# Attention stage of an audio tower: two batches of four product tiles a pair, head projections in another order

## The reference, cut to what matters

```
xn = LN(LN(h)) * ln_scale                       # h: [32, 250, 64]
Q, K, V = xn @ W_q[h], xn @ W_k[h], xn @ W_v[h] # 8 heads
q2, k2 = sum(Q*Q, -1), sum(K*K, -1)
sqdist = max(q2[..., :, None] + k2[..., None, :] - 2 Q K^T, 0)
out    = exp(-gamma * sqdist) @ V               # no normalisation by row
h      = h + concat_heads(out) @ W_o^T
```

## Time and profile before

| | us |
|---|---|
| median of 3 runs (lowest, highest) | 782.41 (780.72, 784.95) |
| the profiled execution | 780.68 |
| its span, first to last instruction | 778.5 |
| PE busy | 741.2 |
| DVE busy | 579.5 |
| ACT busy | 492.1 |
| POOL busy | 459.6 |

### The profile page before, as it was taken

The page is one execution under the profiler, slowest core; times in us unless marked ns, Lnnn a source line. Parts: engine busy times, 40 slices in busy tenths (PEclk is TensorE's granted clock), DMA queues, the critical chain, the costliest instruction groups (busy, mean ns, idle before and its releaser), DMA issues.

```text
span 778.5 us, 17037 instructions
## 1 busy us (share of the span) xinstructions
PE 741.2 (95%) x5712; PEld 435.2 (56%) x5712; DVE 579.5 (74%) x1474; ACT 492.1 (63%) x993; POOL 459.6 (59%) x620
## 2 busy tenths in 40 slices
PE   2999999999999999999999999999999999999994
PEld 1343356776667667676766666544555554454441
DVE  7676776677677676777767665788888888888864
ACT  1566777777767777777777777554554655545441
POOL 7645314654556445564446542367788788888885
PEclk9999999999999999999999999999999999999997
DMA  6300205455755466454664557000000000000000
GB/s 177 105 2 2 53 3 133 110 123 118 160 120 119 106 140 157 109 123 110 145 143 100 117 124 160 2 2 1 9 13 10 9 9 8 8 16 7 9 7 20
DMA packets 41820, 56.20 MB, mean 72 GB/s; under 512 B 16360, under 2 KB 40680, under 8 KB 41608
## 3 DMA queue, kind: packets, MB, share of 16 engines
q1 hardware_dynamic: 40744, 53.87, 30.0%
q10 hardware_dynamic: 992, 1.26, 0.6%
HBM read 5.06 MB, written 2.43 MB: 10 GB/s over the span
## 4 chain that ended last, share of the span: by engine, by line
PE 82%; DVE 4%; POOL 4%; issue 3%; SPq 3%; ACT 3%; DMA 2%; ACTq 0%; DVEq 0%; POOLq 0%
PE bank L1446 14%; PE bank L1424 13%; PE bank L1316 13%; PE bank L1274 10%; PE bank L1343 8%; PE bank L1345 6%; PE bank L1187 5%; PE bank L1278 2%; PE bank L1177 2%; DMA m<-s2o 1%; PE bank L1471 1%; SPq L333 1%; PE bank L1463 1%; PE bank L1230 1%; ACT cs L624 1%
## 5 line engine op out<-in xcount | busy, mean ns | idle before, releaser
L953 DVE TENSOR_SCALAR prob<-prob,cap_hi,cap_lo 125x500 f32<-125x500 f32 x256 | 152.6, 623 | 84.8 <-ACT prob L668 83.7
L478 POOL TENSOR_TENSOR sq<-sq 125x256 f32<-125x256 f32 x128 | 97.5, 773 | 194.2 <-ACT sq L632 172.3
L668 ACT ACTIVATE prob<-bank 125x500 f32<-125x500 f32 x256 | 149.6, 596 | 56.4 <-PE bank L1345 55.8
L1424 PE MATMUL bank<-cs,w_sb 64*64 64x500 f32 x1024 | 147.1, 580 | 2.2 <-DVE gated L1071 2.0
L1446 PE MATMUL bank<-gated,w_sb 64*64 64x500 f32 x1024 | 148.9, 588 | 0.0
L522 POOL TENSOR_TENSOR gated<-relu,wb 128x500 f32<-128x500 f32 x96 | 120.1, 1253 | 48.0 <-ACT relu L768 45.6
L1071 DVE SCALAR_TENSOR_TENSOR gated<-bank,nb,wb 128x500 f32<-128x500 f32 x160 | 114.8, 727 | 35.2 <-PE bank L1424 35.2
L768 ACT ACTIVATE relu<-bank,b_sb 128x500 f32<-128x500 f32 x96 | 64.7, 673 | 93.2 <-PE bank L1424 93.2
L1424 PEld LDWEIGHTS bank<-cs,w_sb 64*64 64x64 f32 x1024 | 53.1, 133 | 54.7 <-issue 48.2
L632 ACT ACTIVATE sq<-bank 125x512 f32<-125x512 f32 x128 | 75.3, 599 | 3.9 <-POOL sq L478 0.8
L1274 PE MATMUL bank<-wqku_hi,s 128*125 128x512 f32 x192 | 77.1, 401 | 0.0
(11 more groups left out here) (188 smaller groups left out, 1507.1 us busy)
## 6 DMA issues: line engine op xcount, KB each, us to landing
m1o<-cs SPq DMA_DIRECT2D x128, 125.0 KB, 2.4
m<-mlow SPq DMA_DIRECT2D x120, 125.0 KB, 2.3
m1e<-cs SPq DMA_DIRECT2D x112, 125.0 KB, 2.4
out<-res SPq DMA_DIRECT2D x15, 125.0 KB
w_sb<-in_w SPq DMA_DIRECT2D x1, 1024.0 KB
m1e<-m1e SPq DMA_DIRECT2D x8, 125.0 KB, 2.3
xa<-xparts SPq DMA_DIRECT2D x3, 281.2 KB
w_sb<-in_w SPq DMA_DIRECT2D x1, 512.0 KB
```

Of the source, the lines that this page charges most:

```text
L478: gp.tensor_tensor(sq2[q][:, :, :], sq[q][:, :, 0:D // 2], sq[q][:, :, D // 2:D], ALU.add)\
L668: act.activation(prob[v % PROBS][:, :, c, :], bank[5 + n % 3][0:T, 0:C].rearrange("p (h l) -> p h l", h=2), ACT.Exp).then_inc(b_exp, 1)
L953: dve.tensor_scalar(part, part, cap_hi[0:T, h:h + 1], cap_lo[0:T, h:h + 1], ALU.min, ALU.max)\
L1424: last = pe.matmul(up_bank(g)[cols, 0:C], w1_sb[rows, g, cols], cs1[q % 3][rows, :], start=True, stop=True)
```

## The change

The order of units becomes the list UNIT_ORDER, by position and no longer by number: 8, 0, 1 in slot 1; 2, 10, 3 in slot 2; 4, 5; 6, 7; 9, 12; 11, 14; 13, 15 in slots 3 to 7. Products run in two batches of four slots each, 16 calls and 32 records a batch: the first four slots at the end of slot 4, the last four in slot 1 of the next step between its two scores. The transposes of the row sums stand right behind the batch of slot 4, and DVE's last two sums and its `stack_rows` at the end of slot 4. POOL's norm scales of the next pair, all seven small operations, move from behind the adds to their front (for steps from 1 on); DVE aggregates in slot 0. The ring `prob` has 6 slots. The start of ACT's `evac_y` moves from the end of slot 0 to slot 1.

```
-            return bank[2 + UNIT_BANKS[k]]
+            return bank[2 + UNIT_BANKS[UNIT_ORDER.index(k)]]
+        def ev_count(p, k):
+            return 16 * p + (k if p == 0 else UNIT_ORDER.index(k)) + 1
         def units(v):
-            return range(0) if v == 0 else range(3 * (v - 1), 3 * v) if v < 3 else range(2 * v, 2 * v + 2)
+            return UNIT_ORDER[slice(0, 0) if v == 0 else slice(3 * (v - 1), 3 * v) if v < 3 else slice(2 * v, 2 * v + 2)]
...
 # POOL
-            def first_scales(p):
+            def b_scales(p):
...
-            def second_scales(p):
-                n = 7 * p
...
+            def b_tokens(p):
+                gp.wait_ge(b_inv, 7 * p + 7)
                 centred(p, b_hc)
...
             def step_b(p, j, old2, old, new, ln):
                 if p == 0:
-                    first_scales(0)
-                    second_scales(0)
+                    b_scales(0)
+                    b_tokens(0)
+                if p > 0 and ln:
+                    b_scales(p + 1)
                 if new:
                     for k in range(8):
                         q = k % 2
-                        gp.wait_ge(b_ev, 16 * p + k + 1)
+                        gp.wait_ge(b_ev, ev_count(p, k))
                         wait(gp, b_red, 8 * p + k - 1)
                         gp.tensor_tensor(sq2[q][:, :, :], ...)
-                    if ln:
-                        first_scales(p + 1)
                     gp.wait_ge(b_red, 8 * p + 8)
...
                 if ln:
-                    second_scales(p + 1)
+                    if p == 0:
+                        b_scales(p + 1)
+                    b_tokens(p + 1)
 # ACT
-                    wait(act, b_pv, 8 * (p - 1) + v - 3)
-                    act.activation(prob[v % PROBS][:, :, c, :], ...)
+                    wait(act, b_pv, 8 * (p - 1) + v + 1 - PROBS)
+                    act.activation(prob[(8 * (p - 1) + v) % PROBS][:, :, c, :], ...)
...
                         if old:
                             exps(v, c)
+                        if v == 1 and c == 0 and old2:
+                            evac_y(p - 2, 1)
                         for k in rest[:1]:
                             unit(p, j, k, unit_bank(k))
                         rest = rest[1:]
-                    if v == 0 and old2:
-                        evac_y(p - 2, 1)
+                    for k in rest:
+                        unit(p, j, k, unit_bank(k))
+                    if new and v == 4:
+                        round_rows(p)
                     if v == 4 and old:
                         evac_y(p - 1, 0)
-                    for k in rest:
-                        unit(p, j, k, unit_bank(k))
-                    if new and v == 5:
-                        round_rows(p)
 # DVE
                 def unit(k):
-                    if 2 <= k < 10:
+                    if 2 <= k < 8:
                         square_sum(p, k - 2)
...
-                    if new and v == 5:
+                    if new and v == 4:
+                        square_sum(p, 6)
+                        square_sum(p, 7)
                         stack_rows(p, j)
                     if ln and v == 0:
                         norm_stats(p + 1, b_ln)
-                    if ln and v == 1:
                         norm_aggr(p + 1, b_ln)
 # PE
                         if old:
                             scores(v, c)
+                        if v == 1 and c == 0 and old2:
+                            for n in range(4, 8):
+                                for hh in range(2):
+                                    products(p - 2, n, j, hh)
                         if rest:
                             unit(rest.pop(0))
                     for k in rest:
                         unit(k)
-                    for n in (v - 2, v - 1) if v % 2 == 0 else ():
-                        for hh in range(2):
-                            if v == 0 and old2:
-                                products(p - 2, n + 8, j, hh)
-                            if v > 0 and old:
+                    if v == 4 and old:
+                        for n in range(4):
+                            for hh in range(2):
                                 products(p - 1, n, o, hh)
...
-                    if new and v == 5:
+                    if new and v == 4:
                         rows_b(p)
...
                 if p == PAIRS + 1:
-                    for n in (6, 7):
+                    for n in range(4, 8):
...
+UNIT_ORDER = (8, 0, 1, 2, 10, 3, 4, 5, 6, 7, 9, 12, 11, 14, 13, 15)
-UNIT_BANKS = (0, 1, 2, 0, 1, 2, 0, 1, 0, 2, 1, 2, 0, 2, 1, 2)
+UNIT_BANKS = (0, 1, 2, 1, 0, 2, 1, 2, 0, 1, 2, 0, 1, 2, 1, 0)
-PROBS = 4
+PROBS = 6
```

More of the change, by code:

```diff
@@ L324, in spread @@
             def spread(p, j, u):
-                sp.wait_ge(b_ev, 16 * p + 9 + 2 * u)
+                sp.wait_ge(b_ev, ev_count(p, 8 + 2 * u))
                 wait(sp, b_sc, 16 * (p - 1))
@@ L459, in second_scales @@
                 gp.tensor_tensor(inv[:, 6, :], inv[:, 1, :], inv[:, 5, :], ALU.mult).then_inc(b_inv, 1)
-                gp.wait_ge(b_inv, n + 7)
+            def b_tokens(p):
+                gp.wait_ge(b_inv, 7 * p + 7)
                 centred(p, b_hc)
@@ L618, in unit @@
             def unit(p, j, k, src):
-                act.wait_ge(b_pj, 16 * p + k + 1)
+                act.wait_ge(b_pj, ev_count(p, k))
                 if is_g(k) and p > 0:
@@ L666, in exps @@
                     act.wait_ge(b_sc, n + 1)
-                    wait(act, b_pv, 8 * (p - 1) + v - 3)
-                    act.activation(prob[v % PROBS][:, :, c, :], bank[5 + n % 3][0:T, 0:C].rearrange("p (h l) -> p h l", h=2),
+                    wait(act, b_pv, 8 * (p - 1) + v + 1 - PROBS)
+                    act.activation(prob[(8 * (p - 1) + v) % PROBS][:, :, c, :], bank[5 + n % 3][0:T, 0:C].rearrange("p (h l) -> p h l", h=2),
                                    ACT.Exp).then_inc(b_exp, 1)
@@ L897, in low_part @@
             def low_part(p, j, k, src):
-                dve.wait_ge(b_ev, 16 * p + k + 1)
+                dve.wait_ge(b_ev, ev_count(p, k))
                 if p > 0:
@@ L951, in caps @@
                     dve.wait_ge(b_exp, 16 * (p - 1) + 2 * v + 2)
-                    part = prob[v % PROBS][:, hh, :, :]
+                    part = prob[(8 * (p - 1) + v) % PROBS][:, hh, :, :]
                     dve.tensor_scalar(part, part, cap_hi[0:T, h:h + 1], cap_lo[0:T, h:h + 1], ALU.min, ALU.max)\
@@ L1316, in products @@
                     last = pe.matmul(bank[1][64 * c:64 * c + 64, 0:L], u_sb[jj][:, 2 * b + c, h * D:(h + 1) * D],
-                                     prob[v % PROBS][:, hh, c, :], start=h == 0, stop=h == H - 1)
+                                     prob[(8 * p + v) % PROBS][:, hh, c, :], start=h == 0, stop=h == H - 1)
                 if hh == 1:
@@ L1348, in unit @@
                 def unit(k):
-                    held = [n for n in range(k) if UNIT_BANKS[n] == UNIT_BANKS[k]]
+                    held = [n for n in UNIT_ORDER[:UNIT_ORDER.index(k)] if unit_bank(n) is unit_bank(k)]
                     if not held:
@@ L1355, in unit @@
                     else:
-                        pe.wait_ge(b_ev, 16 * p + held[-1] + 1)
-                    if k == 0:
+                        pe.wait_ge(b_ev, ev_count(p, held[-1]))
+                    if k == UNIT_ORDER[0]:
                         pe.wait_ge(b_s1, p + 1)
```

## The result

| | before | after |
|---|---|---|
| median, us | 782.1 (780.72 to 784.95, 4 runs) | 790.68 (789.15 to 790.83, 4 runs) |
| profiled execution, us | 780.68 | 790.59 |
| its span, us | 778.5 | 788.7 |
| PE busy, us | 741.2 | 733.5 |

The changed kernel takes 1.0099 times as long (95% interval 1.0076 to 1.0123): 0.8 to 1.2% slower. The forecast was 791. The kernel before has one run more here than in the table ahead of the prediction, hence 782.1.

A forecast was written before the change was run, and what follows sets the result against it. PE's order of issue was taken to bound the kernel. Terms -6.1 (batch edges), -4.2 (row DMA), +18.2 (wait for sums), +1.5 (stage end) gave +9.4 us, 791.8 on the median, stated as 791; 8-in-10 range 775 to 799.

The forecast's parts named there:

- What bounds the stage: Attention step: PE's order of issue is the clock, busy 24.45 of 24.46 us; other engines count only where PE waits.
- The chain of the sums: Scales, adds, squares, caps and sums in series delay the row transposes; PE waits 1.3 us a step, 18.2 in 14 steps.
- Collisions of caps and adds: DVE caps beside POOL adds take 0.96 instead of 0.53 us; with or without, the sums' last series differs some 0.6.
- term a: Product batches on PE: 32 fewer batches save 0.19 us of edges each, 6.1 us in all, within 0 to 6.4.
- term b: First score of a step: PE's wait for the row DMAs behind spread 1 goes, 4.2 us in all, at most 4.2.
- I take 24.45 as the period without a wait: Attention step before the change: undisturbed period, from which all row DMA waits together came to 4.2 us.
- the bank of unit 3: Reuse of PE's banks in the new order, 5 behind 3: costs nothing or under 0.1 us.
- I count it at nothing: Step 1, without residuals or a first batch: no wait for the sums added there.
- The end of the stage: Step 16 and tail: the moved half batch no longer covers PE's wait, which grows 0 to 1.9 us; 1.5 taken.
- about as large as the savings: Rival: wait ahead of the transposes is 0.6 us a step, total -0.4 us, time 782; chance 0.20.

The follow-up runs named there:

- e1: Changed kernel with DVE's norm statistics and aggregation of the next pair moved to the front of slot 0; 782.92 us, ratio 1.0004 to the kernel before.
- e2: Changed kernel with DVE's sums 1 to 6 one unit earlier in its order; 779.73 us, ratio 0.9962 to the kernel before.
- e6: Changed kernel with the row transposes and the split of the rows two items later, behind slot 5's first unit; 775.39 us, ratio 0.9913 to the kernel before.
- e9: e5 with e8's edit of step 1, but batches, transposes' place and tail as before the change; 773.90 us, ratio 0.9875 to the kernel before.
- e10: e8 with the row transposes two items later, as in e6; 761.98 us, ratio 0.9727 to the kernel before.
- e5: Changed kernel with both early norm statistics (e1) and early sums (e2); 771.01 us, ratio 0.9854 to the kernel before.
- e8: Changed kernel with the edits of e5 and e7, and in step 1 POOL's scales behind the adds; 765.95 us, ratio 0.9790 to the kernel before.
- e7: Changed kernel with the last pair's products 4 and 5 back in slot 6 of step 16; 788.76 us, ratio 1.0080 to the kernel before.
- e3: Kernel before with only the two batches of four slots and the ring of six; 822.33 us, ratio 1.0513 to the kernel before.

## Why the prediction was right, point by point

**What bounds the stage.** PE's order of issue was its clock before, and PE's wait for the sums decides after. Right, shown by e1, e2 and e6, each of which changes only order and moves the time with that wait.

**The chain of the sums.** The trace follows it closely. With 0 at the start of unit 8 (315.56 in the step shown), forecast and found: first add 3.2 and 3.2; square of unit 2 4.0 and 4.05; end of slot 2's second exponential 5.1 and 5.1; sum 1's end 6.7 to 7.2 and 7.1; sum 2's end 7.8 to 8.35 and 8.2; sums ready 13.4 to 13.95 and 13.6. One step was loose: the items listed for ACT ahead of slot 0's last exponential add up to 8.4 us and not to 8.7. In the trace POOL's scales start at -0.25, not at -0.7, and end at 3.3, so that the 3.2 came out by the 0.3 allowed for a cap. DVE and POOL in that step:

```profile
322.25 0.41 DVE L900 TENSOR_REDUCE qk<-sq 125x8 f32<-125x256 f32 x1
322.58 0.41 DVE L948 TENSOR_TENSOR z<-bank,h_all 125x256 f32<-125x256 f32 x1
323.02 0.43 DVE L951 TENSOR_TENSOR h_all<-bank,z 125x256 f32<-125x256 f32 x1
323.36 0.41 DVE L900 TENSOR_REDUCE qk<-sq 125x8 f32<-125x256 f32 x1
...
326.01 0.63 DVE L958 TENSOR_SCALAR prob<-prob,cap_hi,cap_lo 125x500 f32<-125x500 f32 x1 [0.60 <-ACT prob L673]
326.56 0.41 DVE L900 TENSOR_REDUCE qk<-sq 125x8 f32<-125x256 f32 x1
```

```profile
318.78 2.23 POOL L483 TENSOR_TENSOR sq<-sq 125x256 f32<-125x256 f32 x3
322.80 0.74 POOL L483 TENSOR_TENSOR sq<-sq 125x256 f32<-125x256 f32 x1 [1.78 <-DVE qk L900]
327.12 0.89 POOL L483 TENSOR_TENSOR sq<-sq 125x256 f32<-125x256 f32 x1 [0.75 <-DVE qk L900]
328.54 0.32 POOL L487 TENSOR_TENSOR qkw<-qk,gneg 125x64 f32<-125x64 f32 x1 [0.53 <-DVE qk L900]
```

Sum 1 at 322.25 ends at 322.66 and releases the add at 322.80; the residuals stand between it and sum 2. The wait is 1.36 to 1.37 us, forecast 1.3.

**Collisions of caps and adds.** Smaller than their bound. Where the chain had 0 to 0.6 us for them, the last caps took 0.63 and 0.53 and the last add 0.89: some 0.3 in all. The mean cap fell from 629 ns before to 551, both over steps 3 to 15. The Trainium skill's sentence in the GPSIMD Engine Reference, section Key points, on interfaces shared with VectorE fits the lengthened rows (0.63 beside an add, 0.53 alone); it does not say how much, no row shows whether a cap is one of the VectorE instructions that it names, and no run here took the collisions away. Their part is read from the trace, not shown by experiment.

**Edges of batches (term a): too small.** I gave a batch 0.19 us, from the two gaps at its ends. The size of the batch inside was off as well: 32 records take 3.52 us (312.04 to unit 8 at 315.56), not twice the 1.84. A batch less is worth 0.30 to 0.35: 2 x (1.84 + 0.19) - (3.52 + 0.19) = 0.35 by the gaps, and (24.12 - 23.52) / 2 = 0.30 by the shortest period of e9 and the mean of e10. 32 batches give some 10 us, not 6.1.

**The row DMA (term b): too small.** 4.2 us was the sum of the waits that exceeded the common one. With 24.12 as the undisturbed period it is 14 x (24.75 - 24.12) = 8.8 us; the weight loads' wait is 8.3. The step of the prediction that failed is "I take 24.45 as the period without a wait".

**What PE waits besides.** I put the bank of unit 3 at under 0.1 us; in slot 3, unit 5, which follows unit 3 in its bank, starts 0.31 behind the record ahead of it and its second record 0.34 later, so some 0.2 us are lost there a step. The loss is gone in e1 and e5 and stays in e2, so it hangs on the late scales.

**The steps together.** From 24.75 the forecast went to 24.75 - 0.38 - 0.30 + 1.3 = 25.37; measured 25.13. The two terms of gain were short by some 0.5 a step, the wait, with the bank and a slower start of the scores behind the transposes, by 0.3.

**Step 1: missed.** "I count it at nothing" was wrong. POOL's scales stand ahead of the adds there too, without the products' batch that covers them in other steps; PE lost 2.5 us, and by my estimate 1 to 1.5 more by the lower clock. With a 16-record batch less than before, the step still takes 1.9 us longer, so the scales cost nearly 4 us there. e8, which differs in this step by the scales' place and the earlier statistics and sums, takes 3.95 us less than the changed kernel; e9 has this wait no more either.

**The end of the stage.** 1.5 forecast. The step is 2.55 longer and has 1.8 more work of one half batch, taken from step 15; 0.8 is its own. e7 gives back 1.5, by the ratios and by the spans from the attention's start. The size is right within 1 us.

**The sum.** The gains were too small by some 8 us, step 1 by 4 the other way, the waits by 4. The attention starts 0.9 us later with the same work; over all twelve traces this start lies anywhere from 108.4 to 111.2 us, so the change need not be its cause. The largest term, 18.2 against 18.9 us, was right by its mechanism. That +9.4 met +10.2 in the span was luck, and so in part was the clear sign: with the gains as measured and all else as forecast the sum is -10 - 8.8 + 18.2 + 1.5 = +0.9 us, the rival "about as large as the savings". What made it clearly slower are things that I had at nothing or nearly so: step 1, unit 5's bank and the slower start of the scores.

## What to carry to other kernels

When work on the bounding engine is merged into a longer block, follow what is late behind it item by item in each engine's own order: here six reductions placed one unit further down on an engine busy for 72% cost the stage about as much (0.87 us a step, by e2) as the merge gave it. A period read as undisturbed may hold a wait that comes in every round; compare the gap with the same pair of instructions elsewhere, and look at the weight loads' waits too. And a wait can be filled as well as shortened: moving the consumer behind two independent items was worth three quarters of repairing the chain, and both together, with the edits of step 1 and of the end, gave the fastest kernel.

## What the runs showed of the hardware

PE's waits of 1.4 us left the granted clock at 1.00. In step 1 it fell to 0.50 behind 2.5 us with nearly no work, and the matmul records ahead of and behind the fall took 0.39 and 0.62 us. e3, with waits of 1.98 to 2.4 us in every step, had 0.93 in the window shown and 0.72 in another of 6 us, and 1.00 throughout others of its steps. I had not expected the size of what the fall costs: 1 to 1.5 us behind 2.5 us of wait in step 1, and some 11 us behind 38 us of waits in e3, both estimates. Further, 32 product records in a row take 3.52 us and 16 take 1.84, so that part of the cost of a batch lies inside it and in no gap.
